# New instruction orders in the first cross-attention stage of a small Perceiver on Trainium2

## The chip, the cores and the metric

One NeuronCore of a Trainium2 chip runs the whole kernel. The metric is the device time in microseconds (us) of one execution, as the median of several runs. The core has five engines with a queue each that run at the same time and meet only at semaphores: TensorE (PE, its weight loads shown as PEld), VectorE (DVE), ScalarE (ACT), GpSimd (POOL) and SyncE (SP), which here issues the DMAs.

## What is computed

Thirty-two sequences of 32 latent rows (512 wide) pass six blocks with residuals. The first is a cross-attention onto 257 context rows (384 wide) plus the latents themselves, 8 heads of 64, keys normalised by their root mean square:

```python
def _L0_xattn_ref(x, latents, mask, ...):
    xn = layernorm(x, ln_x_g, ln_x_b)            # x: the context (32, 257, 384)
    ln = layernorm(latents, ln_l_g, ln_l_b)      # (32, 32, 512)
    q = ln @ Wq.T
    kv = concatenate([xn @ Wkv.T, ln @ Wlkv.T], axis=1)
    ...                                          # split into 8 heads
    qn = rmsnorm(q, qn_g) * SCALE
    kn = rmsnorm(k, kn_g)
    attn = softmax(where(mask, einsum('bhid,bhjd->bhij', qn, kn), -max))
    out = einsum('bhij,bhjd->bhid', attn, v)
    return out @ Wo.T + bo
```

Then come a self-attention over the sequence, a small mixture of low-rank experts, a second cross-attention, a polynomial attention and a mixture of eight feed-forward experts. The change lies in the first block alone.

## The kernel before

The kernel is a row of stages with a barrier between them: latents, **cross0** (the stage of the change), middle, cross1, poly, experts. Float32 products are made on TensorE from pairs of float16 tiles, a "high" part (the value rounded) and a "low" part (what is left), so almost every tile is followed by two elementwise instructions: a copy to float16 and a subtraction.

cross0 handles one batch element b per step of a software pipeline written out by hand. `STEPS` runs from -2 to 38; in step s each engine works on pieces of elements from s+2 down to s-7, in an order that is fixed for each engine by a list of `if on(s - k): piece(s - k)`. The order of an engine's queue is that list; nothing reorders it later. A half of the context rows, 128, is index 0, the other index 1. The life of an element b, with the step it falls in:

- Step b-2: VectorE `stats` (L745 to L752: two bn_stats, two aggregates, a tensor_scalar of 2 elements that adds epsilon). GpSimd `power` (L699, L702) makes the inverse deviation.
- Step b-1: ScalarE `norm` (L883, two activations) writes the normalised rows y; `rows_high` (L905) copies them to float16. TensorE `turn_context` (L1013) transposes them, ScalarE `affine` (L892) and `context_high` (L899) make the turned float16 context.
- Step b: GpSimd `context_low` (L707) its rest, `gather_keys` (L724, L725) brings the latents' keys. TensorE `keys(b, 0, k)`, ScalarE `square(b, 0)` (L911), VectorE `squares(b, 0)` (L756, the sums by head).
- Step b+1: `keys(b, 1, k)`, `square` and `squares` of the other half; GpSimd `rms(b, i)` (L716 and the power L718) for each half; VectorE `key_scale(b, i)` (L762); TensorE `turn_key` (L1032); ScalarE `key_high` (L917) and VectorE `key_low` (L770). GpSimd `rows_low` (L711) subtracts the float16 rows from y, 128x768.
- Step b+2: TensorE `scores` (L1045, L1050), VectorE `softmax_max` (L776), ScalarE `exps` (L925), VectorE `softmax_scale` (L780 reciprocal, L783 two tensor_scalars of 128x256 float32, SBUF to SBUF, in place) and `tail_scale` (L787), TensorE `turn_probs` (L1060) and `turn_tails` (L1066), ScalarE `probs_high` (L930) and `tail_high` (L936), VectorE `probs_low` (L792) and `tail_low` (L798). Then TensorE `mix(b, 0)`: the probabilities times the context rows, for the first half of the heads, into PSUM tile pP; ScalarE `mix_high(b, 0)` (L947) and VectorE `mix_low(b, 0)` (L804) bring it to float16.
- Step b+3: TensorE `mix(b, 1)`, into the same pP, and VectorE `mix_low(b, 1)`. ScalarE's `mix_high(b, 1)` stands as the last piece of step b+2 in its own list.
- Later: `outputs`, `out_high`, `out_low` (L1100 to L1111, L953, L811) and the value weights. A few instructions that fold the layer norm's gain into the value weights (`fold_scale`, `fold_sum`, `fold_high`, `fold_low`) run in steps 0 to 4 only.

`power(b)` waits until `norm(b-1)` is done; `norm(b)` waits for `rows_low(b-2)`, whose source it overwrites; `mix(b, 0)` waits for `rows_low(b)`. `rows_high(b)` waits for `norm(b)` and `mix(b-4, 1)`. TensorE's order, which the change leaves alone, is: outputs, mix(s-3, 1), scores(s-2), keys(s-1, 1), turn_context(s+1), turn_key(s-1, 0), keys(s, 0), between whose three parts turn_probs(s-2) and turn_tails(s-2) stand, mix(s-2, 0), turn_key(s-1, 1).

Of the kernel before, what the change touches and what calls it, by code (L numbers as in the profile page):

```python
# [600 lines left out]
def cross0(st):  # L601
# [9 lines left out]
    with ExitStack() as c:  # L611
# [32 lines left out]
        on = lambda b: 0 <= b < B  # L644
# [43 lines left out]
        @block.gpsimd  # L688
        def _(pool):
            pool.memset(ones[:, :], 1.0).then_inc(sig["c0_const"], 1)  # L690
            pool.memset(minus[:, :], 0.0).then_inc(sig["c0_const"], 1)
            pool.wait_ge(sig["c0_const"], 2)
            pool.memset(minus[0:2, :], -WS).then_inc(sig["c0_const"], 1)

            def power(b):
                pool.wait_ge(sig["c0_stat"], 5 * b + 5)
                if b:
                    pool.wait_ge(sig["c0_norm"], 2 * b)
                pool.tensor_tensor(rs[:, :, 0:1], mv[:, :, 2:3], mhalf[:, 0:2].unsqueeze(2), ALU.pow).then_inc(sig["c0_pow"], 1)  # L699
                pool.wait_ge(sig["c0_pow"], b + 1)  # L700
                for i in range(2):
                    pool.tensor_scalar(rs[:, i, 1:2], rs[:, i, 0:1], mv[:, i, 0:1], -1.0, ALU.mult, ALU.mult).then_inc(sig["c0_rstd"], 1)  # L702

            def context_low(b):
                u = b % 2
                pool.wait_ge(sig["c0_zhi"], b + 1)
                pool.tensor_tensor(LT[u][:, 1, :, :], z[:, :, :], LT[u][:, 0, :, :], ALU.subtract).then_inc(sig["c0_zlo"], 1)  # L707

            def rows_low(b):
                pool.wait_ge(sig["c0_yhi"], b + 1)  # L710
                pool.tensor_tensor(yb[:, b % 4, 1, :, :], y[b % 2][:, :, :], yb[:, b % 4, 0, :, :], ALU.subtract)\  # L711
                    .then_inc(sig["c0_ylo"], 1)

            def rms(b, i):
                pool.wait_ge(sig[f"c0_ss{i}"], b + 1)
                pool.tensor_scalar(ss[i][:, :], ss[i][:, :], HD0 / (HD0 * WS * WS), 1e-16 * HD0, ALU.mult, ALU.max).then_inc(sig[f"c0_ms{i}"], 1)  # L716
                pool.wait_ge(sig[f"c0_ms{i}"], b + 1)
                pool.tensor_tensor(rn[i][:, :], ss[i][:, :], mhalf[:, 0:H0], ALU.pow).then_inc(sig[f"c0_rn{i}"], 1)  # L718

            def gather_keys(b):  # L720
                u = b % 2
                if b >= 2:
                    pool.wait_ge(sig["c0_s"], b - 1)
                pool.tensor_copy(khat[u][:, :, :, FULL:FULL + S], KL[:, :, :, b * S:(b + 1) * S]).then_inc(sig["c0_tail"], 1)  # L724
                pool.tensor_copy(khat[u][:, :, :, KEYS - 1:KEYS], KR[:, :, :, b:b + 1]).then_inc(sig["c0_tail"], 1)  # L725

            for s in STEPS:
                if on(s - 1):
                    rows_low(s - 1)
                    rms(s - 1, 0)  # L730
                if on(s):
                    context_low(s)
                    gather_keys(s)
                if on(s - 1):
                    rms(s - 1, 1)
                if on(s + 2):
                    power(s + 2)

        @block.vector
        def _(dve):  # L740
# [33 lines left out]
            def softmax_max(b):  # L774
                dve.wait_ge(sig["c0_s"], b + 1)
                dve.tensor_reduce(nm[:, :], pS[:, :, 0:KEYS], AX.X, ALU.max, negate=True).then_inc(sig["c0_nm"], 1)  # L776
# [23 lines left out]
            def mix_low(b, g):  # L800
                dve.wait_ge(sig[f"c0_uhi{g}"], b + 1)
                at = slice((b % QUAD) * S, (b % QUAD + 1) * S)
                to = U[b // QUAD % 2][:, :, g, :, :, at]
                dve.tensor_tensor(to[:, 1, :, :, :], pP[:, 0:XK * P].rearrange("p (k h n) -> p k h n", k=XK, h=HG),  # L804
                                  to[:, 0, :, :, :], ALU.subtract).then_inc(sig[f"c0_ulo{g}"], 1)

            def out_low(p):
                n, k = p // CK, p % CK
                dve.wait_ge(sig["c0_ohi"], p + 1)
                to = XT[:, :, k, n * P:(n + 1) * P]  # L810
                dve.scalar_tensor_tensor(to[:, 1, :], pO[:, FULL:FULL + P], 1.0 / WS, to[:, 0, :],  # L811
                                         ALU.mult, ALU.subtract).then_inc(sig["c0_olo"], 1)
# [24 lines left out]
            for s in STEPS:  # L837
                if on(s - 7):
                    out_low(s - 7)
                if on(s - 3):  # L840
                    mix_low(s - 3, 1)
                if on(s - 1):
                    key_scale(s - 1, 0)
                if on(s - 2):
                    softmax_max(s - 2)
                if on(s + 2):
                    stats(s + 2)
                if on(s - 2):
                    softmax_scale(s - 2)
                if on(s - 1):  # L850
                    squares(s - 1, 1)
                if on(s - 2):
                    tail_scale(s - 2)
                if on(s - 1):
                    key_low(s - 1, 0)
                if on(s - 2):
                    probs_low(s - 2)
                if on(s - 1):
                    key_scale(s - 1, 1)
                if on(s):  # L860
                    squares(s, 0)
                if on(s - 2):
                    mix_low(s - 2, 0)
                    tail_low(s - 2)
                if on(s - 1):
                    key_low(s - 1, 1)
                if s == 0:
                    shifts()
                if 0 <= s < XK:
                    fold_sum(s)  # L870
                if 0 <= s - 2 < XK:
                    fold_low(s - 2)

        @block.scalar
        def _(act):
            def norm(b):
                u = b % 2
                act.wait_ge(sig["c0_rstd"], 2 * b + 2)
                if b >= 2:
                    act.wait_ge(sig["c0_T"], b - 1)  # L880
                    act.wait_ge(sig["c0_ylo"], b - 1)
                for i in range(2):
                    act.activation(y[u][:, i, :], cx[u][:, i, :], ACT.Identity, bias=rs[:, i, 1:2], scale=rs[:, i, 0:1])\  # L883
                       .then_inc(sig["c0_norm"], 1)
# [16 lines left out]
            def rows_high(b):  # L901
                act.wait_ge(sig["c0_norm"], 2 * b + 2)
                if b >= 4:
                    act.wait_ge(sig["c0_u1"], b - 3)
                act.activation(yb[:, b % 4, 0, :, :], y[b % 2][:, :, :], ACT.Copy).then_inc(sig["c0_yhi"], 1)  # L905
# [14 lines left out]
            def exps(b):  # L920
                act.wait_ge(sig["c0_nm"], b + 1)
                if b:
                    act.wait_ge(sig["c0_pt"], b)
                for g in range(2):
                    act.activation(pr[:, g, :], pS[:, g, 0:KEYS], ACT.Exp, bias=nm[:, g:g + 1], scale=1.0,  # L925
                                   accum_out=rsum[:, g:g + 1]).then_inc(sig["c0_exp"], 1)
# [38 lines left out]
            for s in STEPS:  # L965
                if on(s + 1):
                    norm(s + 1)
                if on(s - 2):
                    exps(s - 2)
                if on(s - 1):  # L970
                    square(s - 1, 1)
                if on(s + 1):
                    rows_high(s + 1)
                if on(s - 1):
                    key_high(s - 1, 0)
                if on(s - 2):
                    probs_high(s - 2)
                if on(s + 1):
                    affine(s + 1)
                if on(s):  # L980
                    square(s, 0)
                if on(s - 2):
                    mix_high(s - 2, 0)
                    tail_high(s - 2)
                if on(s - 1):
                    key_high(s - 1, 1)
                if on(s - 6):
                    out_high(s - 6)
                if on(s + 1):
                    context_high(s + 1)  # L990
                if on(s - 2):
                    mix_high(s - 2, 1)
                if s == 0:
                    act.wait_ge(sig["c0_bias"], 1)
                    act.activation(shift, pS[0:TAIL, 0, :], ACT.Copy, scale=-1.0 / WS).then_inc(sig["c0_shift"], 1)
                if 0 <= s < XK:
                    fold_scale(s)
                if 0 <= s - 1 < XK:
                    fold_high(s - 1)
# [1952 lines left out]
```

## Time and profile before

| | us |
|---|---|
| median of 3 runs (1716.01 to 1716.78) | 1716.01 |
| the profiled execution | 1715.14 |
| its span, first to last instruction | 1713.0 |
| softmax_max, the first and the last of 32 | 136.6 and 481.6 |

| engine | busy us | share of the span | instructions |
|---|---|---|---|
| TensorE | 1494.7 | 87% | 19391 |
| VectorE | 1170.4 | 68% | 2695 |
| ScalarE | 942.9 | 55% | 2018 |
| GpSimd | 673.1 | 39% | 824 |

The shares are means over stages that differ; cross0, from about 106 to 502 us, is to be read by itself. The mean granted TensorE clock of the run is 0.948 of full speed, 1.00 in the quiet part of cross0. In a timeline each row is one instruction, or a few alike in direct sequence: its start, its duration (of all of them together), the engine, the line, what it writes and reads, and in brackets the idle time before it with the instruction that ended it. Two neighbouring instructions of an engine overlap a little in the records, as the second starts while the first drains.

### The profile page before, as it was taken

To read this page: it belongs to the slowest core of one execution; us is meant where nothing else is said; L and a number is where in the kernel's file an instruction comes from. 1 tells how busy PE (TensorE), PEld (TensorE's weight loads), DVE (VectorE), ACT (ScalarE), POOL (GpSimd) and SP (SyncE) were. 2 spreads that over 40 slices of the span, in tenths; PEclk is the share of its full clock that TensorE was granted. 3 is DMA by queue.
4 is the path that set the end of the run, shared out by engine and by line. 5 is a ranking of instruction groups with operands and counts; after the bars stand their busy time and mean duration, and the time that the engine had idled before them with its cause. 6 is when DMAs were issued, how large, how long until landed. Compare 5 with 4: busy or idle time off the path is not lost. (4 is left out here: it accounts for less than half of the span.)

```text
span 1713.0 us, 48118 instructions
## 1 busy us (share of the span) xinstructions
PE 1494.7 (87%) x19391; PEld 1033.9 (60%) x19391; DVE 1170.4 (68%) x2695; ACT 942.9 (55%) x2018; POOL 673.1 (39%) x824
## 2 busy tenths in 40 slices
PE   6967999999957898699999998899972899989997
PEld 3534566666635676466666665355541678777875
DVE  7858888888846887588888886477775754454441
ACT  5657888888733444266666664133333555555552
POOL 4547777877712111112222221356541333323332
PEclk9989999999978999699999998899995899999999
DMA  6121111111140000022211110300002865565412
GB/s 236 38 66 33 39 43 48 48 39 47 53 177 3 2 2 1 32 88 89 88 52 40 40 40 5 154 8 14 8 14 81 296 191 152 138 191 154 126 33 72
DMA packets 51312, 127.62 MB, mean 75 GB/s; under 512 B 8144, under 2 KB 20784, under 8 KB 51041
## 3 DMA queue, kind: packets, MB, share of 16 engines
q1 hardware_dynamic: 46066, 112.64, 20.0%
q0 software_dynamic: 5008, 11.64, 3.6%
q8 instruction: 170, 2.79, 0.7%
q14 instruction: 68, 0.56, 0.1%
HBM read 110.83 MB, written 15.68 MB: 74 GB/s over the span
## 5 line engine op out<-in xcount | busy, mean ns | idle before, releaser
L106 PE MATMUL e_pGU<-XT,WB 128*128 128x128 f16 x1344 | 232.7, 222 | 15.3 <-issue 10.1
L108 PE MATMUL e_pGU<-XT,WB 128*128 128x128 f16 x1344 | 232.5, 222 | 4.0 <-issue 4.0
L107 PE MATMUL e_pGU<-XT,WB 128*128 128x128 f16 x1344 | 232.6, 222 | 0.0
L2634 DVE SCALAR_TENSOR_TENSOR WB<-raw,WB 128x1024 f16<-128x1024 f32 x96 | 116.3, 1231 | 79.7 <-ACT WB L2785 79.7
L106 PEld LDWEIGHTS e_pGU<-XT,WB 128*128 128x128 f16 x1344 | 133.8, 100 | 22.6 <-issue 20.2
L108 PEld LDWEIGHTS e_pGU<-XT,WB 128*128 128x128 f16 x1344 | 133.8, 100 | 2.6 <-issue 2.6
L107 PEld LDWEIGHTS e_pGU<-XT,WB 128*128 128x128 f16 x1344 | 133.7, 100 | 1.5
L2615 POOL TENSOR_TENSOR XT<-e_mf,XT 128x256 f16<-128x256 f32 x84 | 59.0, 703 | 166.7 <-ACT XT L2799 166.6
L718 POOL TENSOR_TENSOR crn<-css,mhalf 128x8 f32<-128x8 f32 x64 | 105.8, 1654 | 5.3
L2785 ACT ACTIVATE WB<-raw 128x1024 f16<-128x1024 f32 x96 | 97.9, 1044 | 14.8 <-PE e_pY L108 13.9
L2752 DVE SCALAR_TENSOR_TENSOR e_mf<-e_pGU,e_sg 128x256 f32<-128x256 f32 x84 | 35.3, 421 | 84.3 <-ACT e_sg L2797 84.2
L1906 ACT ACTIVATE dpr<-dpS,dnm 128x257 f32<-128x257 f32 x128 | 58.9, 473 | 57.3 <-DVE dnm L1815 57.3
L1762 POOL TENSOR_TENSOR dLT<-ctxin,dLT 128x768 f16<-128x768 f32 x16 | 26.3, 1645 | 128.7 <-DVE dthrice L1825 128.7
L106 PE MATMUL cpP<-cPT,raw 128*128 128x128 f16 x384 | 69.1, 222 | 8.1 <-DVE raw L804 2.5
L1762 POOL TENSOR_TENSOR KL<-ctxin,KL 128x768 f16<-128x768 f32 x15 | 24.7, 1645 | 130.2 <-DVE dthrice L1825 130.2
L106 PE MATMUL cpK<-W,cLT 128*128 128x512 f16 x192 | 74.3, 387 | 0.3 <-POOL cLT L707 0.3
L107 PE MATMUL cpK<-W,cLT 128*128 128x512 f16 x192 | 73.8, 384 | 0.0
L108 PE MATMUL cpK<-W,cLT 128*128 128x512 f16 x192 | 73.7, 384 | 0.0
L2799 ACT ACTIVATE XT<-e_mf 128x256 f16<-128x256 f32 x84 | 35.0, 417 | 69.8 <-DVE e_mf L2752 69.8
L107 PE MATMUL cpP<-cPT,raw 128*128 128x128 f16 x384 | 68.5, 220 | 0.0
L108 PE MATMUL cpP<-cPT,raw 128*128 128x128 f16 x384 | 68.4, 220 | 0.0
L2797 ACT ACTIVATE e_sg<-e_pGU 128x256 f32<-128x256 f32 x84 | 31.7, 378 | 64.7 <-PE e_pGU L108 63.8
(569 smaller groups left out, 5291.6 us busy)
## 6 DMA issues: line engine op xcount, KB each, us to landing
raw<-in_WE SPq DMA_DIRECT2D x96, 512.0 KB, 4.8
raw<-in_W SPq DMA_DIRECT2D x37, 512.0 KB, 4.6
ctxin<-in_ctx SPq DMA_DIRECT2D x32, 384.0 KB, 3.3
ctxin<-in_ctxT SPq DMA_DIRECT2D x32, 384.0 KB
cv<-vlat SPq DMA_DIRECT2D x32, 96.0 KB
X<-in_x SPq DMA_DIRECT2D x8, 256.0 KB, 8.8
vlat<-vl SPq DMA_DIRECT2D x8, 256.0 KB, 2.0
dv<-vrem SPq DMA_DIRECT2D x128, 0.8 KB
```

Of the source, the lines that this page charges most:

```text
L106: pe.matmul(out, lh, rh, start=first, stop=False, skip_group_check=shared)
L107: pe.matmul(out, lh, rl, start=False, stop=False, skip_group_check=shared)
L108: return pe.matmul(out, ll, rh, start=False, stop=last, skip_group_check=shared)
L718: pool.tensor_tensor(rn[i][:, :], ss[i][:, :], mhalf[:, 0:H0], ALU.pow).then_inc(sig[f"c0_rn{i}"], 1)
L1762: pool.tensor_tensor(LT[u][:, 1, :, :], xT[u][:, :, :], LT[u][:, 0, :, :], ALU.subtract).then_inc(sig["d_xlo"], 1)
L1906: act.activation(pr[:, g, :], pS[:, g, 0:SC], ACT.Exp, bias=nm[:, g:g + 1], scale=SCALE, accum_out=rsum[:, g:g + 1]).then_inc(sig["d_exp"], 1)
L2615: pool.tensor_tensor(mT[:, 1, 2 * g:2 * g + 2, :], mf[g % 2][:, :].rearrange("p (a n) -> p a n", a=2), mT[:, 0, 2 * g:2 * g + 2, :], ALU.s ...
L2634: dve.scalar_tensor_tensor(WB[w][:, 1, a], ring[n][:, :], WS, WB[w][:, 0, a], ALU.mult, ALU.subtract)\
L2752: dve.scalar_tensor_tensor(mf[g % 2][:, :], pGU[g % 2][:, 2 * T:4 * T], 1.0 / WS, sg[g % 2][:, :], ALU.mult, ALU.mult)\
L2785: act.activation(WB[w][:, 0, a], ring[n][:, :], ACT.Copy, scale=WS).then_inc(sig["e_whi"], 1)
L2797: act.activation(sg[g % 2][:, :], pGU[g % 2][:, 0:2 * T], ACT.Silu, scale=1.0 / WS).then_inc(sig["e_sg"], 1)
L2799: act.activation(mT[:, 0, 2 * g:2 * g + 2, :], mf[g % 2][:, :].rearrange("p (a n) -> p a n", a=2), ACT.Copy)\
```

## The change

Four orders in cross0 are different; no instruction, tile, wait or DMA is added or taken away.

- GpSimd: `rows_low` is no longer the first piece of a step, for element s-1, but stands between `gather_keys(s)` and `rms(s-1, 1)`, for element s+1. The step's first piece is now `rms(s-1, 0)`.
- VectorE: `mix_low(s-3, 1)` moves from ahead of `key_scale(s-1, 0)` to behind `softmax_max(s-2)`.
- ScalarE: `mix_high` of the second half moves from the end of its step to the next one, behind `norm(s+1)` and ahead of `exps`.
- ScalarE: `rows_high(s+1)` moves from behind `square(s-1, 1)` to ahead of it, directly behind `exps(s-2)`.

```diff
@@ GpSimd
             for s in STEPS:
                 if on(s - 1):
-                    rows_low(s - 1)
                     rms(s - 1, 0)
                 if on(s):
                     context_low(s)
                     gather_keys(s)
+                if on(s + 1):
+                    rows_low(s + 1)
                 if on(s - 1):
                     rms(s - 1, 1)
@@ VectorE
                 if on(s - 7):
                     out_low(s - 7)
-                if on(s - 3):
-                    mix_low(s - 3, 1)
                 if on(s - 1):
                     key_scale(s - 1, 0)
                 if on(s - 2):
                     softmax_max(s - 2)
+                if on(s - 3):
+                    mix_low(s - 3, 1)
                 if on(s + 2):
                     stats(s + 2)
@@ ScalarE
                 if on(s + 1):
                     norm(s + 1)
+                if on(s - 3):
+                    mix_high(s - 3, 1)
                 if on(s - 2):
                     exps(s - 2)
+                if on(s + 1):
+                    rows_high(s + 1)
                 if on(s - 1):
                     square(s - 1, 1)
-                if on(s + 1):
-                    rows_high(s + 1)
                 if on(s - 1):
                     key_high(s - 1, 0)
@@
                 if on(s + 1):
                     context_high(s + 1)
-                if on(s - 2):
-                    mix_high(s - 2, 1)
```

## Rows read from the trace of the kernel before

**Rows 1.** Busy time by engine in stretches: start:end, length, PE, PEld, DVE, ACT, POOL, clock, DMA

```profile
270.00:381.00 111.00, 105.42 (x1318) 70.44 (x1312) 93.11 (x222) 92.84 (x201) 87.12 (x111) 1.00 0.16 47
```

**Rows 2.** One line's instructions (durations in ns), and VectorE's timeline: start, us, instruction

```profile
L776 DVE TENSOR_REDUCE cnm<-cpS x32: 742/749/751, 136.6 to 481.6; 128x2 f32<-128x578 f32 x32
...
301.34 0.69 DVE L762 SCALAR_TENSOR_TENSOR ckh<-cpK,crn 128x512 f32<-128x512 f32 x1 [0.41 <-POOL crn L718]
...
302.73 0.56 DVE L804 TENSOR_TENSOR raw<-cpP,raw 128x384 f16<-128x384 f32 x1
303.20 0.47 DVE L798 SCALAR_TENSOR_TENSOR cPTt<-cPTt,cthird,cpS 99x256 f16<-99x256 f16 x1
...
306.30 0.69 DVE L762 SCALAR_TENSOR_TENSOR ckh<-cpK,crn 128x512 f32<-128x512 f32 x1 [0.47 <-POOL crn L718]
306.90 0.75 DVE L776 TENSOR_REDUCE cnm<-cpS 128x2 f32<-128x578 f32 x1
307.57 1.01 DVE L745 BATCH_NORM_STATS2 cbn<-ctxin 128x6 f32<-128x384 f32 x2
...
308.83 0.17 DVE L752 TENSOR_SCALAR cmv<-cmv 128x2 f32<-128x2 f32 x1
308.91 0.16 DVE L780 RECIPROCAL crinv<-crsum 128x2 f32<-128x2 f32 x1
309.10 0.62 DVE L783 TENSOR_SCALAR probs<-probs,crinv 128x256 f32<-128x256 f32 x2
309.63 0.68 DVE L756 TENSOR_REDUCE css<-csq 128x8 f32<-128x512 f32 x1
...
312.42 0.69 DVE L762 SCALAR_TENSOR_TENSOR ckh<-cpK,crn 128x512 f32<-128x512 f32 x1 [0.41 <-POOL crn L718]
...
317.37 0.69 DVE L762 SCALAR_TENSOR_TENSOR ckh<-cpK,crn 128x512 f32<-128x512 f32 x1 [0.46 <-POOL crn L718]
317.98 0.75 DVE L776 TENSOR_REDUCE cnm<-cpS 128x2 f32<-128x578 f32 x1
```

**Rows 3.** GpSimd's timeline in the same step

```profile
302.54 1.65 POOL L711 TENSOR_TENSOR raw<-cy,raw 128x768 f16<-128x768 f32 x1
304.27 0.25 POOL L716 TENSOR_SCALAR css<-css 128x8 f32<-128x8 f32 x1
...
308.16 0.22 POOL L725 COPY khat<-KR 128x8 f16<-128x8 f16 x1
310.40 0.25 POOL L716 TENSOR_SCALAR css<-css 128x8 f32<-128x8 f32 x1 [2.02 <-DVE css L756]
```

**Rows 4.** ScalarE's timeline in the same step

```profile
305.13 1.29 ACT L883 ACTIVATE cy<-ctxin,crs 128x384 f32<-128x384 f32 x2
307.69 0.50 ACT L925 ACTIVATE probs<-cpS,cnm 128x289 f32<-128x289 f32 x1 [1.26 <-DVE cnm L776]
...
308.65 0.59 ACT L911 ACTIVATE csq<-cpK 128x512 f32<-128x512 f32 x1
309.13 0.85 ACT L905 ACTIVATE raw<-cy 128x768 f16<-128x768 f32 x1
```

**Rows 5.** TensorE's timeline in the same step

```profile
302.09 0.66 PE L1032 MATMUL cpKT<-ident,ckh 128*128 128x128 f32 x4
...
304.99 0.56 PE L1050 MATMUL cpS<-khat,XT 64*32 64x289 f16 x24
```

**Rows 6.** Timelines of ScalarE, GpSimd and VectorE near the stage's start, in that order

```profile
115.17 0.84 ACT L899 ACTIVATE cLT<-cz 128x768 f16<-128x768 f32 x1
...
116.09 1.64 POOL L707 TENSOR_TENSOR cLT<-cz,cLT 128x768 f16<-128x768 f32 x1 [2.68 <-ACT cLT L899]
...
116.65 1.10 DVE L752 TENSOR_SCALAR cmv<-cmv 128x2 f32<-128x2 f32 x1
```

**Rows 7.** Timelines of GpSimd and VectorE in the stage cross1

```profile
1060.98 0.43 POOL L1773 TENSOR_TENSOR XT<-dzo,XT 128x128 f16<-128x128 f32 x1 [8.22 <-ACT XT L1923]
...
1061.08 0.74 DVE L1823 TENSOR_SCALAR dpr<-dpr,drinv 128x256 f32<-128x256 f32 x2
```

## The prediction

> **What bounds the kernel now.** The change touches only the stage called cross0, so I first read the table of engine time by stretch for a quiet 111 us of it [rows 1]: TensorE is busy 105.42 of 111.00 us at a full granted clock, VectorE 93.11, ScalarE 92.84 and GpSimd 87.12. No engine has a free ride, but none is full either (records of neighbouring instructions overlap), so the rate is set by a chain that closes on itself once per batch element. The instruction list shows softmax_max 32 times, from 136.6 to 481.6 us [rows 2]; in the quiet part two neighbours stand at 306.90 and 317.98 [rows 2], a period of 11.08 us. I call the start of softmax_max M and measure everything from it.
>
> Then I followed the chain backwards in the timelines by engine. softmax_max (L776) is issued 0.60 behind key_scale(0) (306.30) with nothing between; that waited 0.47 for GpSimd's power, rms(0), whose first instruction is at 304.27 and stands right behind rows_low (302.54, 1.65 us) [rows 2, 3]. Above rows_low, on the same queue, are power and rms(1), and rms(1) began only when VectorE delivered squares(1): GpSimd sat idle 2.02 us before it, at M+3.50 (310.40) [rows 3]. squares(1) (309.63) stands behind max, stats, reciprocal and softmax_scale on VectorE [rows 2]. So the ring is VectorE from key_scale(0) to squares(1), 4.10 us, and GpSimd from rms(1) through power, **rows_low** and rms(0) to the next key_scale(0): 317.37, that is 306.30 + 11.08, less 310.40, 6.98 us. Their sum is the period. rows_low is a large item in that ring, and what it makes is not needed there.
>
> A second ring is nearly as long. From key_scale(1) (301.34) TensorE's turn_key(1) follows at 302.09, and outputs, mix(1) and scores run to 304.99 + 0.56 = 305.55 [rows 2, 5]. softmax_max needs scores, about 0.05 later, so it could have started at 305.60 and started at 306.90: this ring has 1.30 us of slack, and from key_scale(1) to the earliest M is 4.26. key_scale(1) stands at M+5.52 (312.42) [rows 2]; 2.02 of that is rms(1) to key_scale(1).
>
> **The change, part by part.** Nothing is added or removed; 32 rows_low, 32 rows_high, 32 mix_high(1) and 32 mix_low(1) change places. No DMA is moved; SP's queue keeps its order, and its waits (c0_norm, c0_q) count events whose order does not change.
>
> GpSimd, rows_low. It leaves the place before rms(0), which takes 1.73 us (302.54 to 304.27) out of the first ring, and goes before rms(1), for the element two steps ahead. Queued behind it now are rms(1), power (for which ScalarE's norm of the following step waits, with almost a step of room) and rms(0). When can it run there? It needs rows_high, now directly behind exps on ScalarE. exps starts M+0.79 (307.69); the next ScalarE instruction starts M+1.75 (308.65); rows_high takes 0.85 [rows 4] and ends M+2.60. From ScalarE's end to a waiting GpSimd subtraction: 115.17 + 0.84 = 116.01 to 116.09, 0.08 us [rows 6]. So rows_low runs from **M+2.68 to M+4.32**. GpSimd is free by then (its gather ends at 308.16 + 0.22 = M+1.48) [rows 3]. rms(1) can start 1.73 after it, M+4.41, where it starts at M+3.50 now.
>
> VectorE, mix_low(1). It goes from ahead of key_scale(0) to behind softmax_max. It was idle time there (it waits for ScalarE); as an instruction it takes 0.47 of the queue (302.73 to 303.20, its twin mix_low(0)) [rows 2]. That pushes stats, reciprocal, softmax_scale and squares(1) by 0.47, and about 0.08 more since its new input comes at M+0.75 and not M+0.67 (below). softmax_scale goes from M+2.20 to **M+2.75**.
>
> ScalarE. norm goes ahead of mix_high(1). Both must be through before exps. In time from turn_key(1), norm starts at 305.13 - 302.09 = 3.04 now and 2.55 after (0.49 of mix_high(1) is out of its way); it takes 1.29 [rows 4], mix_high(1) another 0.49, so mix_low(1) has its input at M+0.75 and exps, free at M+0.63, still starts at M+0.79. The norms come earlier, but turn_context stands some 2 us later in TensorE's queue and gains nothing: worth zero. rows_high ahead of square(1) delays square(1) from M+1.75 to M+2.49, its result to M+3.1; squares(1) on VectorE asks for it at M+3.28 or later: zero as well.
>
> **Where the parts meet.** rows_low (from M+2.68) and the two instructions of softmax_scale (from M+2.75) now run side by side; before, GpSimd was idle from M+1.48 to M+3.50 and softmax_scale at M+2.20 was alone. What does that cost? Three rows answer. At 116.09 GpSimd's context_low, an instruction of rows_low's form and size, ran for 1.64 us, and VectorE's two-element tensor_scalar L752, which takes 0.17 elsewhere [rows 2], took 1.10: it ended at 117.75, with the subtraction at 117.73 [rows 6]. In a later stage, a pair of tensor_scalars of exactly softmax_scale's form (f32, 128x256, SBUF to SBUF) took 0.74 where 0.62 is usual (309.10 for softmax_scale, same form), beside a 0.43 us GpSimd tensor_tensor begun 0.10 before it [rows 2, 7]. So VectorE's tensor_scalar stands still until GpSimd's SBUF instruction is through, save for the last 0.15 us or so: 0.93 of a remaining 1.08 in the first case, 0.12 of 0.33 in the second. Other VectorE work, bn_stats, reductions and reads of PSUM, shows no such growth.
>
> The Trainium skill (SBUF — State Buffer, section Who interferes with whom) has this as an exclusive lock on a port pair shared by VectorE and GpSimd, which tensor_scalar takes in its two-port modes; the first to issue keeps it for the whole instruction and the other "fully blocks". Taken to the letter the wait would be the whole rest of rows_low, 0.15 more per step, and the result about 1737 us; the rows show a little less and I use them.
>
> For softmax_scale the rest of rows_low is 4.32 - 2.75 = 1.57, so the delay is 1.42. (If its first instruction gets in ahead, GpSimd waits for that one and the second is held instead; its end is M+4.8 both ways.) Sum: softmax_scale ends at 2.75 + 0.62 + 1.42 = M+4.79, where it was M+2.82; squares(1), queued behind, moves from M+2.73 to M+4.73, and rms(1) from M+3.50 to **M+5.50**; later than the M+4.41 that rows_low alone would set. key_scale(1) is at M+7.52, and 4.26 further, by TensorE's ring, the next softmax_max: **period 11.78**. The first ring, freed of rows_low, would allow about 11.53 (squares(0) behind key_scale(1), then rms(0) with 2.03 to key_scale(0)), so scores decides. Check: the ring over scores gets 2.00 longer and had 1.30 slack, +0.70.
>
> The path over probabilities gives the same within 0.1: turn_probs at M+4.85, probs_low at M+6.4 (VectorE's queue), mix(0) at M+7.2, 1.1 later turn_key(1), M+8.3, which is key_scale(1) + 0.75 too.
>
> How many steps: rows_low and softmax_scale meet in steps 2 to 30 of the loop. From the softmax_max of step 3, the second of the 32, to that of step 30 there are 27 periods; in two of them folding work takes the slack and part of the loss is already there. 25 x 0.70 = 17.5 us. Lead-in (rows_low now ahead of power and of rms(1), whose waits there are mostly for DMA and norms), the folding steps and the last three steps, which lose rows_low from the chain: estimated at 0, within 1.5 either way. The profiled execution took 1715.14 for a span of 1713.0, the median of the runs is 1716.01, 0.9 above it; the difference applied to that median: **1716.0 + 17.5 = 1733.5 us**.
>
> **Rivals.** *Nothing collides* (VectorE is not held in softmax_scale, by another mode or by timing). Then rms(1) starts M+4.41, key_scale(1) M+6.43, M' = 10.69: 0.39 less per step, 10 us less, 1706. For it: all the steady rows before show none of this; against: rows 6 and 7 show it for this form. It ends on the other side. TensorE's own floor, 105.42/111.00 of a period or 10.5, lies just under that. Against it too: softmax_scale would have to be untouched in all of some 27 steps.
> *Both halves of softmax_scale get in first.* A lead of some 0.3 us over my times decides it. Then GpSimd waits 0.55, rms(1) at M+4.95, period 11.23, +4 us: 1720, at the edge of no change. Against it: mix_low(1) puts softmax_scale behind rows_low's start.
> *The small tensor_scalar in stats is caught as well* (M+2.49, if rows_low comes 0.2 sooner than worked out). Then reciprocal and softmax_scale follow it one by one: squares(1) at M+5.1, period 12.15, +27 us: 1743.
> *The reorder does nothing*: the rings before close exactly to 11.08, so removing a piece of one must show; I give this nothing of its own.
>
> **Chances.** The forecast (held once per step) 0.70; caught earlier 0.08; both halves first 0.09, split between same and slower; nothing collides 0.13. Range: 1718 to 1743, which leaves out the faster case and takes in lead-in and latency errors of 0.1 us per step. A measurement of this kernel can tell about 0.2%, 3.4 us, from no change. Faster 0.13, same 0.07 (the half share and 0.02 for errors of the sum), slower 0.80.
>
> **What would show it.** softmax_max every 11.7 to 11.9 us; the pair L783 at 2.0 us, not 0.62, or one of its instructions near 1.8; rows_low beginning within 0.1 of it; GpSimd's idle time before rms(1) still waiting for VectorE, about 1.1; ScalarE's wait before exps longer; softmax_max no longer right behind key_scale(0). Wrong if L783 keeps 0.62: then a period near 10.7.

## The result and the profile after

| | before | after |
|---|---|---|
| median of 4 runs, us | 1716.39 (1716.01 to 1718.38) | 1737.18 (1734.04 to 1739.20) |
| the profiled execution, us | 1715.14 | 1734.04 |
| its span, us | 1713.0 | 1731.9 |

The ratio is 1.0115, with a 95% interval of 1.0101 to 1.0130: slower, as forecast, by 20.8 us in the medians and 18.9 us in the spans of the two profiled executions. The forecast was 1733.5, in a range of 1718 to 1743.

The first part of the changed kernel's page already has the sign: VectorE is "busier" by 40.1 us (1210.5, against 1170.4 before) with the same 2695 instructions, and every other engine by at most 3.4. The row of the same 111 us stretch as [rows 1] shows the other side: TensorE 99.13 busy there instead of 105.42, GpSimd 81.77 instead of 87.12, VectorE 102.12 instead of 93.11. An engine that gets more time for the same instructions is not working more; something keeps its instructions from ending. (Columns of the second fence: start:end, length, PE, PEld, DVE, ACT, POOL, clock, DMA share, GB/s.)

```profile
PE 1498.0 (86%) x19391; PEld 1036.9 (60%) x19391; DVE 1210.5 (70%) x2695; ACT 946.3 (55%) x2018; POOL 674.6 (39%) x824
```

```profile
270.00:381.00 111.00, 99.13 (x1198) 65.93 (x1197) 102.12 (x212) 87.85 (x189) 81.77 (x105) 1.00 0.15 46
```

VectorE's and then GpSimd's timeline of one step of the changed kernel show what. The diff adds a line, so L776 of before is L777 here, L783 is L784, and so on; GpSimd's line numbers up to L725 are unchanged.

```profile
304.82 0.76 DVE L777 TENSOR_REDUCE cnm<-cpS 128x2 f32<-128x578 f32 x1 [0.19 <-PE cpS L1051]
305.50 0.55 DVE L805 TENSOR_TENSOR raw<-cpP,raw 128x384 f16<-128x384 f32 x1
...
307.22 0.17 DVE L753 TENSOR_SCALAR cmv<-cmv 128x2 f32<-128x2 f32 x1
307.30 0.16 DVE L781 RECIPROCAL crinv<-crsum 128x2 f32<-128x2 f32 x1
307.49 2.06 DVE L784 TENSOR_SCALAR probs<-probs,crinv 128x256 f32<-128x256 f32 x2
309.48 0.67 DVE L757 TENSOR_REDUCE css<-csq 128x8 f32<-128x512 f32 x1
...
312.26 0.69 DVE L763 SCALAR_TENSOR_TENSOR ckh<-cpK,crn 128x512 f32<-128x512 f32 x1 [0.41 <-POOL crn L718]
...
315.66 0.69 DVE L763 SCALAR_TENSOR_TENSOR ckh<-cpK,crn 128x512 f32<-128x512 f32 x1 [0.20 <-POOL crn L718]
316.54 0.76 DVE L777 TENSOR_REDUCE cnm<-cpS 128x2 f32<-128x578 f32 x1 [0.19 <-PE cpS L1051]
```

```profile
307.50 1.64 POOL L711 TENSOR_TENSOR raw<-cy,raw 128x768 f16<-128x768 f32 x1 [1.43 <-ACT raw L906]
310.24 0.25 POOL L716 TENSOR_SCALAR css<-css 128x8 f32<-128x8 f32 x1 [1.10 <-DVE css L757]
```

softmax_scale (L784) starts at 307.49, rows_low (L711) at 307.50, and the pair takes 2.06 us where it took 0.62 [rows 2]. The pair is two instructions in direct sequence, and only one of them stands still. The durations of the line over 20 steps (min, median, max in ns) say so: the short one has its 342 ns, the long one 1801. It is the first that is held: in the step shown it starts at 307.49 and takes 1.80 us, and the second starts at 309.2 and takes 0.34.

```profile
L784 DVE TENSOR_SCALAR probs<-probs,crinv x40: 342/1001/1801, 202.1 to 426.4; 128x256 f32<-128x256 f32 x40
```

squares(1) (L757) therefore starts at M+4.66 and GpSimd, done with rows_low, waits 1.10 us more for it, rms(1) at M+5.42. The period, 304.82 to 316.54, is 11.72 us against 11.08. softmax_max no longer stands right behind key_scale(0) [rows 2]: it waits 0.19 us for the scores, which is TensorE's ring. The list of waits in the quiet stretch has the same story from TensorE's side (engine, tile and line, what it waited for: us in total, times, longest): the weight loads of turn_probs (L1061) wait for L784 for 15.7 us in ten steps, where they waited 9.3 before.

```profile
ACT cPT L931 <- PE cpP L1061: 16.8, 10, 1.7
PEld cpP L1061 <- DVE probs L784: 15.7, 10, 1.6
POOL raw L711 <- ACT raw L906: 14.3, 10, 1.4
POOL css L716 <- DVE css L757: 11.0, 10, 1.1
```

### The profile page after: what moved, and what is told of

Its sections match the earlier page's. It is cut to its first block and busy times, and to the rows that moved or that the text cites. A ratio compares the mean times of both kernels' runs of the same rounds, so it can differ in the third digit from the quotient of the medians.

```text
span 1731.9 us, 48118 instructions
## 1 busy us (share of the span) xinstructions
PE 1498.0 (86%) x19391; PEld 1036.9 (60%) x19391; DVE 1210.5 (70%) x2695; ACT 946.3 (55%) x2018; POOL 674.6 (39%) x824
## 3 DMA queue, kind: packets, MB, share of 16 engines
q0 software_dynamic: 5008, 11.64, 3.5%
## 5 line engine op out<-in xcount | busy, mean ns | idle before, releaser
L711 POOL TENSOR_TENSOR raw<-cy,raw 128x768 f16<-128x768 f32 x32 | 52.4, 1639 | 46.4 <-ACT raw L906 46.4
```

## The experiments

Two theories ran against each other. **Held port**: a VectorE tensor_scalar and a GpSimd instruction that both work on SBUF cannot run at once, and the step got longer because they now meet. **The queues**: the loss comes from where the pieces stand, rows_low ahead of rms(1) and mix_low(1) ahead of stats, and the long L784 only fills time. The runs below were made in two later sessions, in which the kernel before scattered more (medians 1720.95 over 25 runs and 1718.33 over 16), so times are given as ratios to the kernel before on the same chip, and the periods, which repeat to 0.02 us from step to step (in e4 and e5 single steps differ by up to 0.2), carry the argument.

### e1: softmax_scale through one port

```diff
 # the changed kernel, softmax_scale
-dve.tensor_scalar(pr[:, g, 0:FULL], pr[:, g, 0:FULL], rinv[:, g:g + 1], None, ALU.mult)
+dve.scalar_tensor_tensor(pr[:, g, 0:FULL], pr[:, g, 0:FULL], rinv[:, g:g + 1],
+                         pS[:, g, 0:FULL], ALU.mult, ALU.bypass)
```

> The changed kernel with softmax_scale written so that VectorE reads only one operand from SBUF and writes through one port: a scalar_tensor_tensor whose second input is the score tile in PSUM and is bypassed. The arithmetic is the same. Theory of the held port: rows_low (GpSimd) still starts at M+2.68 (M is the start of softmax_max) beside softmax_scale, but the pair is no longer held: 0.8 to 1.0 us instead of 2.06; rms(1) then waits only for rows_low, M+4.4; period 10.7, about 1706 us. Rival, the queues: the loss comes from rows_low standing ahead of rms(1) and mix_low ahead of stats, and the long softmax_scale only fills time: the period stays at 11.7 and the time at 1735.

Ratio 0.9943 (0.9916 to 0.9971), profiled execution 1707.12 us. The two instructions still start together, and neither is held (VectorE's rows, then GpSimd's):

```profile
295.34 0.88 DVE L784 SCALAR_TENSOR_TENSOR probs<-probs,crinv,cpS 128x256 f32<-128x256 f32 x2
296.13 0.68 DVE L757 TENSOR_REDUCE css<-csq 128x8 f32<-128x512 f32 x1
...
303.38 0.76 DVE L777 TENSOR_REDUCE cnm<-cpS 128x2 f32<-128x578 f32 x1 [0.19 <-PE cpS L1051]
```

```profile
295.35 1.65 POOL L711 TENSOR_TENSOR raw<-cy,raw 128x768 f16<-128x768 f32 x1 [1.43 <-ACT raw L906]
297.08 0.25 POOL L716 TENSOR_SCALAR css<-css 128x8 f32<-128x8 f32 x1
```

M is 292.67 here, so rms(1) starts at M+4.41, straight behind rows_low, and the period is 10.71 (303.38 less 292.67). With all four orders of the change in place and one form of instruction replaced, the kernel goes from 1.15% slower to 0.6% faster. The queues alone would have kept 11.7. This decides between the two.

### e7: the price of that form

```diff
 # the kernel before, with the same edit as e1 in softmax_scale
```

> The kernel before with the one-port form of softmax_scale, to price the form where nothing meets it. The pair took 0.88 us in the changed kernel with this form, 0.26 more than 0.62; it lies in the ring of key_scale(0) to squares(1), so the period should be 11.08 + 0.26 = 11.34, some 7 us slower. If it were faster, the form and not the absent wait would explain the gain of the changed kernel with it.

Ratio 1.0052 (1.0030 to 1.0075). The pair takes 0.87, GpSimd's idle time before rms(1) is 2.29 instead of 2.02 [rows 3], and the period is 11.34 (301.15 to 312.49), as worked out. The form costs time where nothing meets it, so the gain in e1 is that of the missing hold. In e1 the longer form costs the period nothing, since rms(1) there starts behind rows_low and not behind squares(1).

```profile
301.15 0.75 DVE L776 TENSOR_REDUCE cnm<-cpS 128x2 f32<-128x578 f32 x1
...
303.35 0.87 DVE L783 SCALAR_TENSOR_TENSOR probs<-probs,crinv,cpS 128x256 f32<-128x256 f32 x2
...
312.49 0.75 DVE L776 TENSOR_REDUCE cnm<-cpS 128x2 f32<-128x578 f32 x1
```

### e2: the moves of the rows alone

```diff
 # the kernel before
 GpSimd:  rows_low(s - 1) from the front -> rows_low(s + 1) behind gather_keys(s)
 ScalarE: rows_high(s + 1) behind square(s - 1, 1) -> ahead of it
```

> The kernel before with the moves of rows_low (GpSimd) and rows_high (ScalarE) alone; both mix pieces of the second half stay where they were. Held port: softmax_scale is back at M+2.2, both its instructions are issued before rows_low starts at M+2.68, so the pair keeps 0.62 and rows_low waits 0.1 at most. rms(1) at M+4.4 to 4.5, but mix_low(1) ahead of key_scale(0) lets softmax_max start no earlier than 4.25 us after turn_key(1), where scores alone would allow 3.51: period 11.4 to 11.5, about 1725 us. Rival, the queues: the same place of rows_low costs what it costs in the changed kernel, less 0.5 for mix_low: 11.2, 1720.

Ratio 1.0043 (1.0020 to 1.0065). With mix_low(1) in its old place softmax_scale starts 0.47 earlier than rows_low and is all but through when that starts: both keep their length.

```profile
301.75 0.62 DVE L784 TENSOR_SCALAR probs<-probs,crinv 128x256 f32<-128x256 f32 x2
...
305.97 0.69 DVE L763 SCALAR_TENSOR_TENSOR ckh<-cpK,crn 128x512 f32<-128x512 f32 x1 [0.93 <-POOL crn L718]
```

```profile
302.22 1.65 POOL L711 TENSOR_TENSOR raw<-cy,raw 128x768 f16<-128x768 f32 x1 [2.14 <-ACT raw L906]
303.95 0.25 POOL L716 TENSOR_SCALAR css<-css 128x8 f32<-128x8 f32 x1
```

The period is 11.41 (299.55 to 310.96). It is longer than before without any hold, for the reason given with the expectation: rms(1) is 0.9 later, behind rows_low, and the other ring, which now counts, still has mix_low(1) ahead of key_scale(0). The rival had 11.2, and misses by ten times the spread of the period.

### e3: the moves of the mix pieces alone

```diff
 # the kernel before
 VectorE: mix_low(s - 3, 1) ahead of key_scale(s - 1, 0) -> behind softmax_max(s - 2)
 ScalarE: mix_high(s - 2, 1) at the end of the step -> mix_high(s - 3, 1) behind norm(s + 1)
```

> The kernel before with the moves of mix_high(1) (ScalarE) and mix_low(1) (VectorE) alone; rows_low stays first on GpSimd. Held port: nothing meets (GpSimd idle while softmax_scale runs), pair 0.62; but the ring of key_scale(0) to squares(1) and rms(1), power, rows_low, rms(0) grows by the place of mix_low(1), 0.47 to 0.55: period 11.6, about 1731 us. Rival: without the move of rows_low there is no loss, 11.1, 1716.

Ratio 1.0040 (1.0018 to 1.0061), period 11.56 (301.52 to 313.08). rms(1) comes 0.47 later (M+3.97) and drags rows_low, rms(0) and key_scale(0) along; before key_scale(0) VectorE now sits idle 1.77 us. The period was as expected, the time was not: some 7 us by the ratio instead of 15. From the first softmax_max to the last, 27 of the 31 periods lost 0.47 each, but the first, with the folding work in it, took 11.49 instead of 14.14, and the last three about 0.7, 0.7 and 0.1 less than before: those are steps in which, as I read the orders, ScalarE's folding work and key_scale no longer stand behind the second mix; no run separates that. The first softmax_max came 2.2 us later, for a reason not looked into, so that the last is 10.8 late (492.38 instead of 481.56), and not 7. Part of what is left may be the clock, which is not shown: the runs of e3 have a median granted clock of 0.946, those of the kernel before in that session 0.944. e2 has the same pattern: its last softmax_max is 10.8 late as well, and its ratio says 7.

So each half of the change costs by itself, 0.33 and 0.47 us a step; together, had they merely added up, they would have given 11.9, had they only made way for each other 10.7 (e1). What they gave, 11.72, is the hold.

### e6: rows_low in two halves

```diff
 # the changed kernel, rows_low: one instruction of 128x768 becomes two of 128x384
-pool.tensor_tensor(yb[:, b % 4, 1, :, :], y[b % 2][:, :, :], yb[:, b % 4, 0, :, :], ALU.subtract)
+for i in range(2):
+    pool.tensor_tensor(yb[:, b % 4, 1, i, :], y[b % 2][:, i, :], yb[:, b % 4, 0, i, :], ALU.subtract)
```

> The changed kernel with rows_low as two instructions of 128x384, about 0.94 us each (by the 0.70 us of a 128x256 and the 1.64 us of a 128x768 subtraction). If the two engines take turns at each instruction, the first half holds softmax_scale's first instruction, the second half its second: the pair takes 2.2 us, as long as before or longer, period 11.8 to 11.9, about 1740 us. If VectorE, once it is let in, runs both of its instructions, the pair takes 1.4 us and the second half comes behind it; rms(1) then waits for rows_low until M+5.2: period 11.5, about 1730 us. Rival, no port: the split changes only GpSimd's own time, pair 0.62.

Ratio 1.0100 (1.0065 to 1.0134), period 11.64. The durations of softmax_scale's and rows_low's instructions over 20 steps:

```profile
L785 DVE TENSOR_SCALAR probs<-probs,crinv x40: 929/999/1077, 202.1 to 424.3; 128x256 f32<-128x256 f32 x40
```

```profile
L712 POOL TENSOR_TENSOR raw<-cy,raw x40: 911/936/963, 202.2 to 424.2; 128x384 f16<-128x384 f32 x40
```

Where one of VectorE's instructions stood still for 1.45 us, now both do, for about 0.65 each: the engines take turns, instruction by instruction. The total, 1.99 for the pair, is 0.2 less than I had for that case and the period 0.2 less: GpSimd loses next to nothing in taking turns (0.94 for a half, as worked out from other sizes), and VectorE's instruction is let in shortly before GpSimd's ends, twice instead of once.

### e4, e5 and e8: rows_low out of the way

The place behind gather_keys was a poor one only because the element asked for is the one whose input ScalarE is just making. `rows_low(s)` has had its input since the step before.

```diff
 # e4, from the changed kernel         # e5, from the changed kernel
     context_low(s)                        context_low(s)
     gather_keys(s)                   +    rows_low(s)
-if on(s + 1):                              gather_keys(s)
-    rows_low(s + 1)                  -if on(s + 1):
+    rows_low(s)                      -    rows_low(s + 1)
 # e8: GpSimd's order of e5 in the kernel before, nothing else changed
```

> The changed kernel with rows_low for element s, not s+1, in the same place behind gather_keys(s): its input was made a step earlier, so it needs no wait and starts right behind gather_keys, about M+1.3, and ends about M+2.9, when softmax_scale has just begun. Held port: the pair is held 0.1 or less, rms(1) waits for squares(1) at M+4.0, period 10.3 (near TensorE's own 10.1 to 10.5), about 1695 us, faster than the kernel before. Rival, the queues: rows_low is still ahead of rms(1) and mix_low ahead of stats, no gain over the changed kernel beyond the 1.1 us it waited for ScalarE: 11.2 or more, 1720.

> The changed kernel with rows_low for element s between context_low(s) and gather_keys(s) on GpSimd. In the run with rows_low behind gather_keys it ran from M+1.19 to M+2.84 and held VectorE's two-element tensor_scalar at M+2.40 for 0.29 us. Here it should run from about M+0.7 to M+2.35, just clear of it; only the small copies of gather_keys then stand beside softmax_scale. Held port: tensor_scalar back at 0.17, pair 0.62 to 0.7, period 10.3 and 7 us less than in that run, some 20 us less than the kernel before. Rival: that run was already at TensorE's own limit (105.42 busy in ten steps, 10.5 each), and the 0.29 us cost nothing: the period stays at 10.57.

> The kernel before with one edit: rows_low(s) between context_low(s) and gather_keys(s); rows_high and both mix pieces stay in their places. softmax_max cannot start earlier than 4.25 us after turn_key(1), since mix_low(1) stands ahead of key_scale(0), and VectorE's small tensor_scalar stands at M+1.93, before rows_low is through at about M+2.35. Held port: that one is held some 0.3 us, rms(1) comes at M+3.5 to 3.9, period 10.5 to 10.9: the moves of the mix pieces are worth 0.2 to 0.6 us a step once rows_low is out of the way, against a cost of 0.47 us a step while it is not. Rival: the mix moves are worth nothing here either, and the period equals that of the kernel with all moves.

| | ratio to before | period, us | L752 / the pair L783, us | first and last softmax_max |
|---|---|---|---|---|
| before | 1 | 11.08 | 0.17 / 0.62 | 136.6 and 481.6 |
| e4 | 0.9913 (0.9883 to 0.9943) | 10.56 | 0.46 / 0.62 | 138.5 and 466.7 |
| e5 | 0.9925 (0.9900 to 0.9951) | 10.42 | 0.33 / 0.62 | 140.2 and 469.1 |
| e8 | 0.9928 (0.9901 to 0.9955) | 10.56 | 0.24 / 0.62 | 138.0 and 471.2 |

All three beat both kernels, by 0.7 to 0.9% of the kernel before (15 us for e4 and 13 for e5, where some 20 were expected of each); which of them is best can't be told from these times. e5's period is the shortest, but e4 is through its last softmax_max 2.4 us earlier. It loses the lead in the steps with folding work: e5 takes 15.18 and 12.52 us for the first two periods, e4 12.75 and 10.20. One collision there is plain: in e5 rows_low, now directly behind context_low, runs beside a folding tensor_tensor of VectorE with two SBUF inputs (L821), and that takes 2.12 us at 152.69, where in e4 it takes 0.88 at 149.87. So a quiet stretch alone does not choose between two orders. In e4 a piece of the hold is left, on the two-element tensor_scalar of stats; in e5 I had expected it gone, and it is smaller, but there. The rows, e4 first (VectorE, GpSimd), then e5:

```profile
290.98 0.46 DVE L752 TENSOR_SCALAR cmv<-cmv 128x2 f32<-128x2 f32 x1
```

```profile
289.77 1.65 POOL L711 TENSOR_TENSOR raw<-cy,raw 128x768 f16<-128x768 f32 x1
```

```profile
295.67 0.33 DVE L752 TENSOR_SCALAR cmv<-cmv 128x2 f32<-128x2 f32 x1
```

```profile
293.98 1.64 POOL L711 TENSOR_TENSOR raw<-cy,raw 128x768 f16<-128x768 f32 x1
295.57 0.41 POOL L724 COPY khat<-KL 128x256 f16<-128x256 f16 x1
```

In e4 rows_low ends at 291.42 and the tensor_scalar at 291.44. In e5 rows_low ends at 295.62, before the tensor_scalar starts, and that is held by the copy behind it, which ends at 295.98; it ends at 296.00. I had put the copies beside softmax_scale and forgotten that rows_low's end, not its start, decides where they lie. Both periods were expected at 10.3, and this hold is nearly all that they missed by. It pushes softmax_scale, squares(1) and rms(1) back; rms(1) starts at M+4.26 in e4 and M+4.13 in e5, and with 2.02 to key_scale(1) and 4.28 and 4.27 from there to the next softmax_max that closes to 10.56 and 10.42. So the ring still sets the period, though TensorE is nearly full, 109.78 of 111.00 us busy in e5; the rival, that e4 was already at TensorE's limit and its hold cost nothing, is out, since the period fell when the hold did.

```profile
270.00:381.00 111.00, 109.78 (x1392) 74.89 (x1387) 100.70 (x238) 99.63 (x214) 92.79 (x116) 1.00 0.17 51
```

e8 needs a single edit of the kernel before and has nearly all of the gain: the ring over rows_low was what held the kernel at 11.08. Its period lies within the 10.5 to 10.9 expected, but rows_low starts 0.01 before softmax_max and is through at M+1.65, not M+2.35. What meets the tensor_scalar, and holds it by 0.07, is the two small copies behind it. The mix moves cost 0.47 a step while rows_low stands in that ring (e3); together with the move of rows_high, which no run separates from them, they are worth 0.14 once it does not (e8 against e5), less than the 0.2 to 0.6 expected: mix_low(1) ahead of key_scale(0) gives the 4.25 us from turn_key(1) to softmax_max (298.97 to 303.22 in e8), and against that stands 0.55 less work ahead of squares(1).

## Why the prediction was right, point by point

*The rings.* Both were read rightly, including the 1.30 us of slack in the one over scores: e1, e2, e3 and e7 came out at 10.71, 11.41, 11.56 and 11.34 where the same sums gave 10.7, 11.4 to 11.5, 11.6 and 11.34. In e4 and e5 they gave 10.3 for 10.56 and 10.42, for want of the hold on the small tensor_scalar.

*Where the parts meet.* rows_low was put at M+2.68 and runs at M+2.68. softmax_scale was put at M+2.75 and runs at M+2.67: norm starts 2.45 behind turn_key(1), not 2.55 (315.46, 313.01), so mix_high(1) is through 0.1 earlier and mix_low(1), at M+0.68, does not wait for it. The end of the pair does not depend on that start, since the end of rows_low sets it; it is M+4.73, against M+4.79 in the sum, because the unheld part was 0.21 us and not 0.15.

*The hold.* 1.44 us (2.06 less 0.62) against 1.42. The two are that close because two small errors cancel: 1.65 of rows_low was left and not 1.57, and the hold was 0.21 shorter than this rest and not 0.15 (0.21 is also what rows 7 gives, and 0.15 rows 6). The two cases in the trace of before [rows 6, 7] were enough. The Trainium skill (SBUF — State Buffer, section Who interferes with whom) says "fully blocks", which in this sum would have been 0.15 more; the traces agree that one of the two is blocked by the other, though in the record the blocked one, at 307.49, starts 0.01 us ahead, and also with its remark that a VectorE instruction with one SBUF input outside the two-port modes does not contend (e1's form, 0.88 beside rows_low and 0.87 alone).

*The sum.* The period came out 11.72 and not 11.78, which is 1.6 us over 27 steps. Over these 27 the stage grew by 17.0 us against the 17.5 of the sum, since one of the folding steps lost 1.1 us and not nothing. The lead-in I had at zero within 1.5 was +1.8 at the first softmax_max (136.6 to 138.4): rms(1) of the first element starts 1.3 later, behind the rows_low now ahead of it (130.33 instead of 129.00), and that makes a folding instruction of VectorE with two SBUF inputs meet GpSimd's context_low, which holds it: 2.02 us for 0.75. The folding instruction before, then after, then context_low after:

```profile
134.52 0.75 DVE L816 SCALAR_TENSOR_TENSOR raw<-W,vecs,raw 128x512 f32<-128x512 f16 x1 [0.58 <-ACT raw L957]
```

```profile
135.85 2.02 DVE L817 SCALAR_TENSOR_TENSOR raw<-W,vecs,raw 128x512 f32<-128x512 f16 x1 [0.58 <-ACT raw L958]
```

```profile
135.68 1.64 POOL L707 TENSOR_TENSOR cLT<-cz,cLT 128x768 f16<-128x768 f32 x1
```

The step after it gave back 0.9 and the tail 0.5. So the terms put at nothing came to +1.6 together by the last softmax_max, just outside the 1.5 allowed, and the 25 quiet periods to 15.8 instead of 17.5; that the total came within 0.5 us of the sum is in part luck. At the end of the stage the changed kernel is 17.9 us late (first low part of the next stage's weights at 521.92 instead of 504.00). The span is 18.9 longer; the last 1.0 us arises in stages whose code is the same. The rest of the 20.8 us between the medians is the scatter of the runs: the profiled execution is the fastest of the changed kernel's four. The mean granted clock of TensorE goes with it, 0.945 in the runs of 1734.04 and 1735.90 us, 0.943 in that of 1738.47 and 0.942 in that of 1739.20, as in the 25 runs of the kernel before in the first of the later sessions, from 1712.34 at 0.949 to 1726.56 at 0.940. In which stages the time goes can't be seen, as only one run has a trace.

*The rivals.* "Nothing collides" was priced at 10.69 and 1706; e1 realises it at 10.71 and 1707 (profiled), so what failed that rival is its condition and not its sum. "Both halves first" did not occur in any of the 27 steps in which the pair and rows_low meet: a lead of 0.01 us was not enough to let even the first of them through ahead of rows_low. The small tensor_scalar of stats was not caught either (0.17 us at 307.22, rows_low 0.28 behind it). TensorE's floor of 10.5 a period was none: e5 runs at 10.42.

## What to carry to other kernels

Before an instruction is moved into another engine's idle time, ask what the neighbour on the shared path does in just that time; here GpSimd's idle 2 us were the very window in which VectorE's tensor_scalars ran alone, and a move that took 1.7 us out of the ring cost 0.64 us a step. An instruction whose duration grows while its count and shape stay the same is the sign. If a piece has to leave a critical ring, give it the element whose input is a step old: it then starts when the engine is free and not when another engine has just finished, which also makes its place choosable.

## What the runs showed of the hardware that I had not expected

That GpSimd and VectorE can take turns instruction by instruction, even with the next instruction of the same engine queued behind: two halves of rows_low held one softmax_scale instruction each, 0.65 us (e6), where the whole held one of them 1.45 and left the other its 0.34. It is not a rule, and the hold goes both ways: near the start of the stage before the change GpSimd's context_low, started at 125.29, took 2.59 us instead of 1.64, while two VectorE instructions with two SBUF inputs ran one behind the other (124.95 and 125.62, 0.75 and 0.74 us), the second at no more than its length elsewhere. It waited through both. Instructions of VectorE with two SBUF inputs were held before the change as well (L821: 2.13 us at 147.59, 0.68 at 159.13), which the prediction's list of work that is not held leaves out.

And how small a thing is enough to hold or be held: a copy of 128x256 float16, 0.41 us, kept a two-element tensor_scalar back by 0.16 us in the quiet steps of e5, and that one stands ahead of the whole of softmax_scale. In e4, e5 and [rows 6] the two-element instruction ended 0.02 us after the other, and in e8 0.02 after a copy of 128x8. It takes 0.17 alone, so 0.15 of it is not added to the wait; of the 0.34 of softmax_scale's first instruction it was 0.2 (it ended at 309.29, rows_low at 309.14).
